# The causal block with the values stationary in four column groups, the mask folded into the maximum, and the rows divided out before they are turned

## The reference

```
h = rmsnorm(x, ln1_w)
q, k, v = heads(h @ wq.T, 4), heads(h @ wk.T, 2), heads(h @ wv.T, 2)
q, k = q * cos + rotate_half(q) * sin, k * cos + rotate_half(k) * sin
scores = einsum('bhtd,bhsd->bhts', q, repeat(k, 2)) / sqrt(16)
scores = where(s <= t, scores, -1e30)
att = softmax(scores)
x = x + einsum('bhts,bhsd->bhtd', att, repeat(v, 2)) @ wo.T
```

## Time and profile before

| | us |
|---|---|
| median of 3 runs | 6219.48 (6199.0 to 6223.66) |
| the profiled execution | 6179.57 |
| its span on the core | 6177.8 |
| PE busy | 5130.0 (83%) |
| DVE busy | 4184.2 (68%) |
| ACT busy | 3919.1 (63%) |
| POOL busy | 3537.1 (57%) |

### The profile page before, as it was taken

How to read it: one execution, slowest core, us unless ns; L and a number is a source line. 1 busy time by engine, 2 the same in 40 slices (tenths; PEclk the granted TensorE clock), 3 DMA queues, 4 the chain that set the end, 5 groups by cost and what they waited for, 6 DMA issues and landing times. The chain is left out here.

```text
span 6177.8 us, 99317 instructions
## 1 busy us (share of the span) xinstructions
PE 5130.0 (83%) x28905; PEld 3048.5 (49%) x28905; DVE 4184.2 (68%) x7201; ACT 3919.1 (63%) x5322; POOL 3537.1 (57%) x3151
## 2 busy tenths in 40 slices
PE   2688888888888888888888888888886999997999
PEld 1344444444444444444444444444444777775777
DVE  2577777777777777777777777777774545555443
ACT  1577777777778777787777877778773222222222
POOL 4677777777777777777777777777772101000111
PEclk9899999999999999999999999999997989898999
DMA  0000000000000000000000000000000000000000
GB/s 11 15 8 11 7 7 7 7 11 7 7 7 9 9 7 7 7 9 9 7 7 7 9 9 7 7 7 9 9 6 8 1 1 1 1 1 16 5 4 6
DMA packets 34157, 45.63 MB, mean 7 GB/s; under 512 B 24473, under 2 KB 24537, under 8 KB 34010
## 3 DMA queue, kind: packets, MB, share of 16 engines
q1 hardware_dynamic: 31962, 43.49, 2.5%
q0 software_dynamic: 2048, 0.14, 0.1%
HBM read 39.40 MB, written 4.19 MB: 7 GB/s over the span
## 5 line engine op out<-in xcount | busy, mean ns | idle before, releaser
L588 PE MATMUL banks<-ident,att 128*128 128x128 f32 x8192 | 1148.7, 287 | 405.4 <-DVE ag L520 244.1
L588 PEld LDWEIGHTS banks<-ident,att 128*128 128x128 f32 x8192 | 945.8, 147 | 999.0 <-DVE ag L520 614.0
L630 PE MATMUL banks<-kT,qT 128*128 128x512 f32 x2048 | 1144.0, 658 | 274.6 <-DVE mx L549 265.1
L390 POOL TENSOR_TENSOR sinb<-sinb,ag 128x1024 f32<-128x1024 f32 x512 | 1281.2, 2505 | 83.7 <-ACT sinb L461 68.4
L540 DVE SCALAR_TENSOR_TENSOR mag<-near,mag 128x512 f32<-128x512 int32 x1024 | 865.7, 850 | 483.2 <-POOL near L406 474.5
L647 PE MATMUL outp<-work,vo 128*64 128x512 f32 x2048 | 1045.0, 635 | 0.0
L647 PE MATMUL outp<-sinb,vo 128*64 128x512 f32 x2048 | 1044.9, 635 | 0.0
L400 POOL TENSOR_SCALAR mag<-mag 128x512 f32<-128x512 f32 x1024 | 689.3, 677 | 565.8 <-DVE mag L540 531.1
L406 POOL TENSOR_SCALAR near<-mag 128x512 int32<-128x512 f32 x1024 | 796.4, 778 | 355.8 <-ACT mag L479 293.8
L479 ACT ACTIVATE mag<-banks 128x512 f32<-128x512 f32 x1024 | 599.2, 592 | 279.8 <-PE banks L630 279.4
L497 DVE TENSOR_TENSOR work<-banks,work 128x1024 f32<-128x1024 f32 x512 | 625.3, 1221 | 188.5 <-ACT work L455 185.5
(11 more groups left out here) (199 smaller groups left out, 7085.9 us busy)
## 6 DMA issues: line engine op xcount, KB each, us to landing
x<-xT_dram SPq DMA_DIRECT2D x128, 256.0 KB, 3.4
xT_dram<-xT SPq DMA_DIRECT2D x8, 256.0 KB, 2.9
out<-hres SPq DMA_DIRECT2D x8, 256.0 KB, 2.6
base<-in_L_tok_turns,idx POOLq DMA_INDIRECT x64, 2.2
wqk<-in_L_attn_Wq SPq DMA_DIRECT2D x64, 16.0 KB
wqk<-in_L_attn_Wk SPq DMA_DIRECT2D x64, 16.0 KB
wqk<-in_L_attn_bq SPq DMA_DIRECT2D x64, 0.2 KB
wqk<-in_L_attn_bk SPq DMA_DIRECT2D x64, 0.2 KB
```

The costliest lines, as they stand in the source:

```text
L390: nc.gpsimd.tensor_tensor(sinb[:, k % RING], sinb[:, k % RING], ag[:, k], ALU.mult).then_inc(tmul, 1)
L588: mm = nc.tensor.matmul(turn_pair(k)[:, c, i * P:(i + 1) * P], att[:, p, 4 * half + i, kt * P:(kt + 1) * P], ident[:], is_transpose=True, ...
L630: nc.tensor.matmul(score_bank(n), qT[:, p, (n // 2) * P:(n // 2 + 1) * P], kT[:, p, (n % 2) * 512:(n % 2 + 1) * 512], start=True, stop=Tru ...
```

## The change

What it does, part by part:

- **Values stationary.** The product with the values is turned round: 32 columns (16 of them zero) of `c_v` are stationary and the 128 columns of a block of `c_prT` are moving. The four heads of a query tile go to rows 0, 32, 64 and 96 of `c_yp`, four groups of 32 columns of the array. PE does it once in four steps, for all four heads of a query tile, at the step n with n - 5 = 3 modulo 4. The result is already turned, so the transposes of the result (L1079) go.
- **Mask and maximum in one.** DVE reads the scores from PSUM and a mask from SBUF, writes the negated sum to `c_pr` and the negated maximum to `c_nm` in one custom instruction (L971 of the new kernel) with a small second one for the accumulated result. The mask matmul (L1053) goes. ACT takes its exponential in place in `c_pr`. A score slot is now free when DVE has read it (`maxed`).
- **Row sums divided out by POOL.** At the end of every step DVE waits for ACT's exponential of the same unit and takes one reciprocal of 128x1; POOL multiplies the unit's weights by it in place, and PE's transposes wait for that (`normed`). DVE's division at the end goes.
- **Copies shared.** Every third copy from `c_pt` to `c_prT` is ACT's, and ACT copies the result `c_yp` to `c_yT` twice a batch.
- **Lags.** Transposes go from 2 to 3 steps behind, the product with the values to 5, the output projection to step 6, the residual to step 7; POOL's `rope` is spread over steps 17 to 27.
- `c_wo` is loaded by four DMAs into 128 rows that POOL has zeroed, where it was one; `c_mask` is fp32 and 1024 wide.

```diff
-        wo = sb("c_wo", [D, D])
+        wo = sb("c_wo", [P, D])
...
-        v = sb("c_v", [P, 2, TB * NKV * HD])
+        v = sb("c_v", [P, 2, TB * NKV, 2 * HD])
         pr = sb("c_pr", [P, 4, S])
-        prT = sb("c_prT", [P, 4, S])
+        prT = sb("c_prT", [P, 2 * NH, S])
...
-        TURN_AT, APPLY_AT = 2, 3
-        NORM_AT = APPLY_AT
-        YT_AT, WO_AT = APPLY_AT + 2, APPLY_AT + 4
...
+        TURN_AT, APPLY_AT = 3, 5
+        OUT_AT, WO_AT, ADD_AT = APPLY_AT, APPLY_AT + 1, APPLY_AT + 2
+        TAIL = ADD_AT + 1
+        ROPE = {17: "q", 19: 0, 21: 1, 23: 2, 25: 3, 27: "k"}
...
+        def by_act(n, g):
+
+            return TURNS_OF.index((n, g)) % 3 == 2
...
+            for h in range(NH):
+                sp.dma_start(wo[32 * h:32 * h + HD, :], woT[h * HD:(h + 1) * HD, :]).then_inc(w_in, 16)
+            sp.wait_ge(w_in, 144)
...
+                for n in range(steps(b)):
+                    if exists(b):
+                        w = (UNITS[n][0] + 1) * P
+                        held(pool, recip, NU * b + n + 1)
+                        nc.gpsimd.tensor_scalar(pr[:, n % 4, 0:w], pr[:, n % 4, 0:w], rs[:, par, n:n + 1], 1.0,
+                                                ALU.mult, ALU.mult).then_inc(normed, 1)
...
-                        if n >= 4 or exists(b - 1):
-                            wait(act, pt_done, use(*turned(*at(b, n, 4))))
                         w = (UNITS[n][0] + 1) * P
-                        nc.scalar.activation(pr[:, n % 4, 0:w], sc[:, score_slot(n), 0:w], ACT.Exp,
-                                             bias=nm[:, par, n:n + 1], scale=1.0,
+                        nc.scalar.activation(pr[:, n % 4, 0:w], pr[:, n % 4, 0:w], ACT.Exp,
+                                             bias=nm[:, par, n:n + 1], scale=-1.0,
                                              accum_out=sm[:, par, n:n + 1]).then_inc(expd, 1)
+                    tb, tn = at(b, n, TURN_AT)
+                    if exists(tb):
+                        for g in range(parts(tn)):
+                            if by_act(tn, g):
+                                wid = min(UNITS[tn][0] + 1 - 4 * g, 4) * P
+                                wait(act, pt_done, turned(tb, tn, g))
+                                wait(act, yd, TB * tb + tn // NH - 1)
+                                nc.scalar.activation(prT[:, tn % (2 * NH), g * 512:g * 512 + wid],
+                                                     bank(tn, g)[:, 0:wid], ACT.Copy).then_inc(pt_sb2, 1)
+                    ob, on = at(b, n, OUT_AT)
+                    if exists(ob) and on in (NU // 2 - 1, NU - 1):
+                        half = on // (NU // 2)
+                        wait(act, yd, TB * ob + on // NH + 1)
+                        wait(act, wd, ob)
+                        nc.scalar.activation(yT[:, half * 512:(half + 1) * 512], yp[:], ACT.Copy).then_inc(yT_sb, 1)
                     if pieces(b) and PIECES.get(n) == "x":
...
                     if exists(b):
+                        w = (UNITS[n][0] + 1) * P
                         wait(dve, sc_done, NU * b + n + 1)
-                        nc.vector.tensor_reduce(nm[:, par, n:n + 1], sc[:, score_slot(n), 0:(UNITS[n][0] + 1) * P],
-                                                AX, ALU.max, negate=True).then_inc(maxed, 1)
+                        if n >= 4 or exists(b - 1):
+                            wait(dve, pt_done, turned(*at(b, n, 4)))
+                        dve.nop(nofuse=True)
+                        nc.vector.tensor_tensor_reduce(
+                            pr[:, n % 4, 0:w], sc[:, score_slot(n), 0:w], mask[:, S - w:S], -1.0, 3.0e38,
+                            ALU.add, ALU.min, nm[:, par, n:n + 1]).then_inc(maxed, 1)
                     if pieces(b) and n + 1 in PIECES and PIECES[n + 1] == "x":
                         scale_tokens(b + 1)
...
-                            what = turned(tb, tn, g)
-                            wid = min(UNITS[tn][0] + 1 - 4 * g, 4) * P
-                            wait(dve, pt_done, use(*what))
-
-                            wait(dve, yd, NU * tb + tn - 3)
-                            nc.vector.tensor_copy(prT[:, tn % 4, g * 512:g * 512 + wid],
-                                                  bank(*what)[:, 0:wid]).then_inc(pt_sb, 1)
-                    if n == NORM_AT and exists(b - 1):
-                        wait(dve, expd, NU * b)
-                        nc.vector.reciprocal(rs[:], sm[:, 1 - par]).then_inc(recip, 1)
-                        wait(dve, recip, b)
-                        wait(dve, yd, NU * b)
-                        nc.vector.tensor_tensor(y[:].rearrange("p t (h d) -> p (t h) d", d=HD),
-                                                yp[:].rearrange("p (n d) -> p n d", d=HD),
-                                                rs[:].unsqueeze(2).to_broadcast([P, NU, HD]),
...
+                            if not by_act(tn, g):
+                                wid = min(UNITS[tn][0] + 1 - 4 * g, 4) * P
+                                wait(dve, pt_done, turned(tb, tn, g))
+                                wait(dve, yd, TB * tb + tn // NH - 1)
+                                nc.vector.tensor_copy(prT[:, tn % (2 * NH), g * 512:g * 512 + wid],
+                                                      bank(tn, g)[:, 0:wid]).then_inc(pt_sb, 1)
+                    if exists(b):
+                        wait(dve, expd, NU * b + n + 1)
+                        nc.vector.reciprocal(rs[:, par, n:n + 1], sm[:, par, n:n + 1]).then_inc(recip, 1)
...
                 if isinstance(item, int):
-                    wait(pe, expd, NU * b + item + 1)
+                    wait(pe, maxed, NU * b + item + 1)
...
                             e = min(c + 512, (qt + 1) * P)
-                            nc.tensor.matmul(s[:, c:e], q_h[:, par, h, qt * P:(qt + 1) * P], k_r[:, par, c:e],
-                                             start=True, stop=True, skip_group_check=True)
-
-                        nc.tensor.matmul(s[:, qt * P:(qt + 1) * P], one[:], mask[:], start=False, stop=True,
-                                         skip_group_check=True).then_inc(sc_done, 1)
+                            mm = nc.tensor.matmul(s[:, c:e], q_h[:, par, h, qt * P:(qt + 1) * P], k_r[:, par, c:e],
+                                                  start=True, stop=True, skip_group_check=True)
+                        mm.then_inc(sc_done, 1)
                         last[score_slot(n)] = (b, n)
                     if n in PIECES and pieces(b):
...
                     if exists(tb):
-                        wait(pe, expd, NU * tb + tn + 1)
+                        wait(pe, normed, NU * tb + tn + 1)
                         for g in range(parts(tn)):
-                            what = turned(tb, tn, g)
-
-                            wait(pe, pt_sb, use(*what) - 3)
+                            dve_moved, act_moved = moved(tb, tn, g)
+                            if by_act(tn, g):
+                                wait(pe, pt_sb2, act_moved - 1)
+                            else:
+                                wait(pe, pt_sb, dve_moved - 2)
                             pe.nop(nofuse=True)
                             for i in range(min(UNITS[tn][0] + 1 - 4 * g, 4)):
-                                mm = nc.tensor.transpose(bank(*what)[:, i * P:(i + 1) * P],
+                                mm = nc.tensor.transpose(bank(tn, g)[:, i * P:(i + 1) * P],
                                                          pr[:, tn % 4, (4 * g + i) * P:(4 * g + i + 1) * P], ident[:])
                             mm.then_inc(pt_done, 1)
-                    if n == YT_AT and exists(b - 1):
...
-                    if exists(ab):
-                        wait(pe, pt_sb, use(*turned(ab, an)))
-                        if an == 0:
+                    if exists(ab) and an % NH == NH - 1:
+                        qt = an // NH
+                        dve_moved, act_moved = moved(ab, an, parts(an) - 1)
+                        wait(pe, pt_sb, dve_moved)
+                        wait(pe, pt_sb2, act_moved)
+                        if qt == 0:
                             wait(pe, v_sb, ab + 1)
-                            wait(pe, ynorm, ab)
+                            wait(pe, w_sb, ab)
+                        if qt == TB // 2:
+                            wait(pe, yT_sb, 2 * ab + 1)
                         pe.nop(nofuse=True)
-                        qt, h = UNITS[an]
                         vpar = par if n >= APPLY_AT else 1 - par
                         for kt in range(qt + 1):
-                            col = kt * NKV * HD + h // (NH // NKV) * HD
-                            mm = nc.tensor.matmul(yp[:, an * HD:(an + 1) * HD], prT[:, an % 4, kt * P:(kt + 1) * P],
-                                                  v[:, vpar, col:col + HD], start=(kt == 0), stop=(kt == qt),
-                                                  skip_group_check=True)
```

(36 more changed lines are left out.)

119 lines of the change are left out of this document (48 added, 71 removed).

## The result

| | before | changed |
|---|---|---|
| median | 6211.18 us | 6004.15 us |
| lowest to highest | 6199.0 to 6223.66 | 5986.29 to 6039.33 |
| the profiled execution's span | 6177.8 | 5984.5 |
| ratio, with its 95% interval | | 0.9674 (0.9623 to 0.9724) |

The kernel is faster by 3.3%. The forecast was 6050 us, 5985 to 6130. In a later measurement, with five rounds on one chip, the ratio was 0.9683 (0.9642 to 0.9723). One of the four executions of experiment 7 took 14851 us, for no reason that a trace shows, and its ratio is formed without that one.

What follows compares the result with a forecast made beforehand. PE was taken to bound the causal block at 103.3 us a batch; steps of 76.4, low clock 4 and late copies 1.6 made 82. Eight batches save 170 us, +2 for DMAs: 6219.5 - 169 = 6050 us, range 5985 to 6130.

Steps and rivals of the forecast that it cites:

- neither clock nor coupling costs anything: Rival for the causal block: no loss to low clock or late copies, 76 us a batch or less, 6000 and below; chance 0.08.
- 39.9 us up: Whole time: the median of the runs shown before lay 39.9 us above the profiled execution, so 6010 became 6050.
- PE is the bound: Causal block before: PE busy for 702 of 723 us, its work 92.8 of 103.3 us a batch, DVE half free.
- Values 32.0 to 10.2 us: Values' product on PE, per batch: four groups side by side take 7.8 us, switches in 8 bursts 2.4, instead of 32.0.
- The step's chain: Each step lasts at least maximum, exponential, reciprocal and hand-overs: 0.99 us at k = 1 to 2.67 at k = 8, 58.6 a batch.
- Step by step, 76.4 us at full clock: Causal block, per batch: each group of four steps takes the longer of chain and PE work, plus pieces joining them; sum 76.4 us.
- The low clock, 4 us a batch, and 1.6 for late copies: Added per batch: half the 8.3 us lost to low clock at a batch's start, and 0.05 us a step for late copies and slots.
- ACT as releaser of PE's transposes: Sign against the forecast: in the trace of after, PE's transposes wait for ACT; no size given.
- POOL as releaser or a clock below 0.9 over the block: Signs against the forecast: PE's transposes wait for POOL, or granted clock under 0.9 because PE waits in each step.
- +2 us for three more DMAs: Start of the block: three more DMA issues, 0.63 us apart, delay DVE's beginning by 2 us.
- The rule on drains: Bursts of the values' product: changing the tiling mode drains TensorE, taken as 0.09 us each way.
- The rule of about 62 ns per matmul: Values' product: microcode of about 62 ns per matmul without hardware decoding would make a pass of four about 0.25 us, not 0.109.

Runs made afterwards that it cites:

- experiment 7: Changed kernel with DVE's reciprocal a step later and ACT's copy ahead of its exponential: 5967.12 us, ratio 0.9628 to the kernel before.
- experiments 1 and 2: Changed kernel with the values' matmuls beyond the first key block in one column group (6118.07 us, ratio 0.987) or in two (6028.38 us, 0.9728).
- experiment 4: Changed kernel with DVE's reciprocal of a unit moved behind the maximum of the next unit: 5955.69 us, ratio 0.9618 to the kernel before.
- experiment 6: Changed kernel with ACT's share of the copies moved ahead of its exponential of the same step: 5977.06 us, ratio 0.9645 to the kernel before.

## Why the prediction was right, and where it was off

The direction, the mechanism and the range held; the gain was 207 us for 169. The measured 6004 us and 76.9 us a batch stand nearer to the rival "neither clock nor coupling costs anything" (76 us or less, 6000 and below), which had 0.08, than to the forecast of 82 us and 6050. Of the 46 us between forecast and median, 22 have nothing to do with the change: I set the figure for the profiled execution 39.9 us up, and it was 17.9. The block came 200 us shorter for 170, and the blocks ahead happened to be 15 us longer. Point by point:

- **PE is the bound.** Held in the main. The PE work that experiments 1 and 2 put back came out in the time (17.3 of 17.9 and 6.1 of 6 us a batch). But experiment 4 took no work from PE and gave 3.2 us a batch: in the steps of k = 8 without a burst DVE's chain had set the pace, 2.78 us, where they now take 2.42 to 2.48.
- **Values 32.0 to 10.2 us.** Held: the burst of k = 6 was to take 0.22 x 6 + 0.3 = 1.6 and takes 1.44 with the switch behind it and 1.54 with both; the groups beside each other are worth 138 us. From 12 passes of four at 0.109 us, 0.23 remains for both switches. I had 0.3, which my own rows (0.09 twice and 0.05) do not give: they say 0.23.
- **The step's chain.** The steps of k = 8 are 2.78 us for a chain of 2.67 and a forecast of 2.7 to 2.9; the custom operation takes 1.23 as the reduction did. That it binds beside PE was right, though I had it bind at k = 3 and, with a projection, at k = 4 and 5 alone, and for k = 6 to 8 took PE's work as the longer: there the steps without a burst ran at the chain's pace, and the step with the burst took its 4.47 us on top. Taking the chain away gave 25.7 us; in batch 6 it was 2.9 less at k = 6 to 8, 1.1 less at k = 3 and 1.1 more at k = 1, 2 and 4.
- **Step by step, 76.4 us at full clock.** The sum held by luck. Batch 6, at a granted clock of 1.00, took 76.3, but with errors both ways: k = 1, 2, 4 and 5 together took some 4 us less than I had, k = 3, 6, 7 and 8 some 4 more. Over seven batches it is (5397.9 - 4859.4) / 7 = 76.9 us from residual to residual, in a row of the kind of the earlier trace rows, with two turns of the loop in it, which I had not thought of, and a last batch that prepares no next one:

```profile
L993 DVE TENSOR_TENSOR x<-c_yp,x x8: 671/692/693, 4859.4 to 5397.9; 128x512 f32 x6, 128x512 f32<-128x512 f32 x2
```

  The four steps of k = 8 took 5085.09 - 5072.21 = 12.9 us for my 11.6: PE's transposes waited for a copy of ACT, late behind its exponential, and experiment 6 took 1.1 of these 1.3 us away.
- **The low clock, 4 us a batch, and 1.6 for late copies.** This is the term that was mis-sized. I took the clock of before as given, 8.3 us lost, and halved it on the ground that steps which wait for the chain hide a slower PE. But the clock itself rose: 0.98 over the block, and 0.94 in 30 us from a batch's start where the earlier trace rows had 0.72. By the working that gave 8.3, some 1.5 us a batch are lost. PE waited 12.6 / 8 = 1.6 us a batch for late copies, as allowed for, but all of it at k = 8, where it is in the 76.3 already; I had added it to the 76.4.
- **ACT as releaser of PE's transposes.** I had named this as a sign that the forecast is wrong, and it came: 16 times, 12.6 us. It did not overturn the forecast, since it is 1.6 us a batch. The other such signs, POOL as releaser or a clock below 0.9 over the block, did not come.
- **+2 us for three more DMAs.** Did not come. DVE begins 4720.56 - 4713.37 = 7.2 us after the first issue, as it did before (7.1). The four issues of `c_wo` stand 0.49 us apart, and DVE begins 2.9 us after the last of them, where in the kernel before it began 4.2 us after the last issue; which of the DMAs makes the difference is open:

```profile
4716.15 1.96 SPq L801 DMA_DIRECT2D c_wo<-in_woT  x4
```

```profile
4720.56 0.34 DVE L913 TENSOR_SCALAR c_wqk<-c_wqk,lnw 64x256 f32<-64x256 f32 x1 [7.47 <-DMA c_wo<-in_woT]
```

- **The rule on drains** (the Trainium skill, "TensorEngine Tiling (Array Packing)", Key Properties): the trace agrees, 0.10 us from the last transposes' stream to the burst's first load. **The rule of about 62 ns per matmul** (the Trainium skill, "TensorE: Matmul & The Clock Gate", Wait — 56ns, not 53.3ns?) does not bind here: 48 matmuls took 1.44 us, 30 ns each, and the four of a pass start within 0.02 us of one another.

The gain of 200 us in the block can be followed through the kernels that were run, between the maxima themselves: 810.4 before, 765.4 with the clock at 1.00 (45.0 less), 748.2 with the whole change but one column group (17.2 less), 610.0 with four (138.2 less). The 17.2 hold the masks, the two transposes of the result, the new order of waits and a clock that is 0.98 again, all at once, and none of these was tried alone in the kernel before. Undone in the changed kernel, the mask's part is worth 13.

## What to carry to other kernels

Where a product has few output channels, put them on the stationary side and give each head a column group: in fp32 a pass of four groups took 0.109 us here, the time of one, and the price was a switch of about 0.1 us each way, so gather them in bursts. When an engine gets a wait on the result of its own step, put it behind the first work of the next step: it moved a few lines and gave another 25.7 us here, an eighth of what the change gave in the block, and moving a copy that another engine's ring waits for gave half as much, though only 0.6 us in batch 6. Price each part of a composite change by itself: here one part carried over two thirds of it, one was free, and one was worth 0.2%. And compare a stretch without disturbances (here batch 6, which repeats to 0.03 us), step by step, before a sum is taken as proof: three times here a sum came out as reckoned by chance, with its parts wrong (the 76.4 us of the steps, the 1.9 of the masks, the 12.6 of the copies).

## What the runs showed of the hardware

- Four fp32 matmuls in four column groups, each with its own moving data, run beside one another: four start within 0.02 us, the next four 0.11 us later, and 48 take 1.44 us, or 1.54 with both switches. In one group the 18 of a stretch of 24 that must queue cost 1.94 us more, 0.11 each.
- A kernel that streams more came out faster: the block has a granted clock of 0.93 (the levels are 1.2 and 2.4 GHz) and 810.4 us with 16 columns moving in each of the values' matmuls, and 1.00 and 765.4 us with 128. These 45 us are more than several of the edits that saved work gave.
- POOL's 256 multiplications of 128 to 1024 columns (0.37 to 1.13 us) beside a DVE that reads PSUM did not slow it: the custom operation took 1.23 us, as the reduction did, and leaving them out changed the block by 1.8 us.
- At a turn of the hardware loop PE stood idle for 3.78 and 3.48 us in the changed kernel, without a wait that the profile shows, and the step took 5.80 us for 2.85.
